# Attention maxima reduced two banks at a time, with four banks for maxima and two for scores

## The reference

```python
q = _split_heads(x @ qw + qb)
k = _split_heads(ctx @ kw + kb)
v = _split_heads(ctx @ vw + vb)
scores = jnp.einsum('bqhd,bkhd->bhqk', q, k) / np.sqrt(D // H).astype(np.float32)
if mask is not None:
    scores = scores + mask
probs = jax.nn.softmax(scores, axis=-1)
out = jnp.einsum('bhqk,bkhd->bqhd', probs, v)
...
h = h @ w + b + residual      # then a layer norm
ca = _mha(input_tensor, ctx_tensor, ctx_attn_mask, ...)   # cross
sa = _mha(x, x, None, ...)                                # self, on the cross result
```

## Time and profile before

| what | us |
|---|---|
| median of three timed runs (2017.12 to 2017.86) | 2017.5 |
| the profiled execution's own time | 2010.88 |
| its span | 2009.2 |
| PE busy | 1782.9 (89%) |
| DVE busy | 1414.8 (70%) |
| ACT busy | 1221.4 (61%) |
| POOL busy | 1217.2 (61%) |
| mean granted TensorE clock | 0.947 |
| DVE reductions of line 711, 1024 of 684 ns | 650.5 |
| ACT exponentials of line 625, 1024 of 601 ns | 571.3 |

### The profile page before, as it was taken

One profiled execution on the slowest core, in us unless ns is written; L12 is line 12 of the kernel. 1 busy time (PEld: TensorE's weight loads), 2 busy tenths in 40 slices (PEclk: granted clock), 3 DMA queues, 4 the chain that ended last, 5 costly groups with the idle time before them and its releaser, 6 DMA issues. The chain is left out here.

```text
span 2009.2 us, 36355 instructions
## 1 busy us (share of the span) xinstructions
PE 1782.9 (89%) x12326; PEld 1320.8 (66%) x12326; DVE 1414.8 (70%) x2786; ACT 1221.4 (61%) x2305; POOL 1217.2 (61%) x1117
## 2 busy tenths in 40 slices
PE   0699699999999999996994999941999999999996
PEld 0355355555555555553543898841999999999995
DVE  5378578878787887885852789863766666666662
ACT  0167467767676776774772554512777777777773
POOL 6644475556657555554435365651778778878875
PEclk9799899999999999998997999965999999999998
DMA  3665356656555665643503022215666766766662
GB/s 91 118 136 106 88 102 137 136 114 143 113 129 98 137 137 113 139 111 69 119 31 113 31 83 88 85 72 177 226 218 216 224 218 216 222 220 216 222 219 39
DMA packets 125197, 274.80 MB, mean 137 GB/s; under 512 B 15802, under 2 KB 57914, under 8 KB 124628
## 3 DMA queue, kind: packets, MB, share of 16 engines
q1 hardware_dynamic: 110708, 253.77, 46.2%
q0 software_dynamic: 14304, 18.72, 4.6%
HBM read 196.50 MB, written 75.92 MB: 136 GB/s over the span
## 5 line engine op out<-in xcount | busy, mean ns | idle before, releaser
L711 DVE TENSOR_REDUCE nz<-ps 128x1 f32<-128x512 f32 x1024 | 650.5, 684 | 215.9 <-PE ps L849 214.0
L625 ACT ACTIVATE spare<-ps 128x512 f32<-128x512 f32 x1024 | 571.3, 601 | 296.9 <-PE ps L859 292.6
L1747 POOL TENSOR_TENSOR u_lo<-u_f,u_hi 128x256 fp32r<-128x256 f32 x273 | 378.8, 1398 | 145.4 <-ACT u_hi L1781 144.0
L1853 PE MATMUL ps_e<-x_hi,we_hi 128*128 128x256 f32 x1092 | 312.8, 286 | 4.9 <-DVE we_lo L1667 4.9
L1853 PE MATMUL ps_e<-x_lo,we_hi 128*128 128x256 f32 x1092 | 305.6, 280 | 0.0
L1853 PE MATMUL ps_e<-x_hi,we_lo 128*128 128x256 f32 x1092 | 305.5, 280 | 0.0
L859 PEld LDWEIGHTS ps<-qst,kst 52*128 52x128 f32 x1024 | 101.7, 184 | 278.1 <-ACT spare L625 192.4
L871 PE MATMUL ps<-spare,vaug 128*32 128x512 f32 x2048 | 275.3, 610 | 0.0
L859 PE MATMUL ps<-qst,kst 52*128 52x512 f32 x1024 | 269.2, 502 | 3.8 <-ACT spare L625 3.5
L849 PE MATMUL ps<-kst,qst 50*128 50x512 f32 x1024 | 263.9, 441 | 9.1 <-issue 8.3
L1707 DVE TENSOR_TENSOR u_f<-ps_e,silu 128x256 f32<-128x256 f32 x273 | 115.1, 422 | 182.5 <-ACT silu L1812 181.3
(11 more groups left out here) (224 smaller groups left out, 3612.3 us busy)
## 6 DMA issues: line engine op xcount, KB each, us to landing
we_raw<-in_experts_w SPq DMA_DIRECT2D x117, 896.0 KB, 4.9
parts_kept<-parts SPq DMA_DIRECT2D x64, 512.0 KB, 3.9
kst<-parts_kept SPq DMA_DIRECT2D x192, 128.0 KB, 4.5
qst<-parts_kept SPq DMA_DIRECT2D x192, 128.0 KB, 5.2
x_raw<-xs SPq DMA_DIRECT2D x39, 259.0 KB, 2.8
maxima<-nsplit SPq DMA_DIRECT2D x64, 128.0 KB, 2.9
x<-sum_tok SPq DMA_DIRECT2D x16, 512.0 KB, 2.7
x_tok<-x SPq DMA_DIRECT2D x16, 512.0 KB, 4.0
```

Source lines behind the costliest of these rows:

```text
L625: act.activation(probs[:, e % 8], ps[:, score_bank(e, par)], ACT.Exp, scale=SCALE).then_inc(exp_made, 1)
L711: dve.tensor_reduce(nz[:, g % 2, place:place + 1], ps[:, max_bank(m, par)], AX.X, ALU.max, negate=True).then_inc(max_made, 1)
L1747: pool.tensor_tensor(u_lo[:, it], u_f[:, q % UPS], u_hi[:, it].bitcast(F32), ALU.subtract).then_inc(ulo_made, 1)
L1853: ins = pe.matmul(ps[:, q % UPS, c * GR:(c + 1) * GR], left, right, start=m == 0, stop=m == len(terms) - 1)
```

## The change

There are four banks for maxima and two for scores. DVE reduces the two heads of a pair in one instruction, which reads two banks and writes two maxima for each query, and raises its semaphore by two. It waits for the second product of the pair.

```diff
-SCORE_BANKS, MAX_BANKS, MISC_BANKS = 3, 3, 1
+SCORE_BANKS, MAX_BANKS, MISC_BANKS = 2, 4, 1
...
             def reduce_max(u, m, par):
-                g, i, qt, half = max_place(m)
+                g, i, qt, _ = max_place(m)
                 if m % 16 == 0 and positive(u * NG + g - 1):
                     dve.wait_ge(nz_turned, u * NG + g - 1)
-                dve.wait_ge(max_mm, u * 64 + m + 1)
-                place = qt * 32 + 2 * half + i
-                dve.tensor_reduce(nz[:, g % 2, place:place + 1], ps[:, max_bank(m, par)], AX.X,
-                                  ALU.max, negate=True).then_inc(max_made, 1)
-                if m % 16 == 15:
+                dve.wait_ge(max_mm, u * 64 + m + 2)
+                place = qt * 32 + i
+                bank = max_bank(m, par)
+                dve.tensor_reduce(nz[:, g % 2, place:place + 3:2], ps[:, bank:bank + 2], AX.X,
+                                  ALU.max, negate=True).then_inc(max_made, 2)
+                if m % 16 == 14:
                     turn_max(u, g)
...
-                for m in range(LEAD):
+                for m in range(0, LEAD, 2):
                     reduce_max(0, m, 0)
...
-                    for m in (2 * s + LEAD, 2 * s + LEAD + 1):
-                        if m < 64:
-                            reduce_max(u, m, par)
-                        elif after:
-                            reduce_max(u + 1, m - 64, 1 - par)
+                    m = 2 * s + LEAD
+                    if m < 64:
+                        reduce_max(u, m, par)
+                    elif after:
+                        reduce_max(u + 1, m - 64, 1 - par)
```

## The result

The changed kernel takes 2061.0 us (median of four, 2060.2 to 2061.7) against 2017.7 before (2017.1 to 2024.7): a ratio of 1.0206, with a 95% interval of 1.0183 to 1.0229. It is slower by 43 us; forecast were 37. Its profiled execution took 2061.66 us with a span of 2059.9, so that the two spans differ by 50.7 us. Of the 50.7 some 7 are luck, as the kernel before took 2010.9 in its profile against a median of 2017.7; in the 13 runs beside e7_turn_late it took 2010.7 to 2020.8.

The account below looks back on a forecast made before the run. PE was taken as the bound, with about 42 us of DVE waits over it. Score waits less DVE waits gave +49 us, less 12 given back, +37 on 2017.5: 2054 us, range for 8 in 10 2028 to 2084.

Parts of the forecast that it names:

- What bounds: In attention, PE is the bound, with about 42 us of DVE waits over the kernel, 2.5 us a period.
- The reductions: On DVE, one reduction over two banks takes 1.21 us (bounds 1.14 and 1.37); some 4 us a period relieved, hidden.
- Maxima with four banks: In attention periods, four banks for maxima take off nearly the whole DVE wait: 2.5 us a period.
- The start: At the start, 34 maxima reduced in pairs in place of singly: about 1 us less.
- Scores with two banks: In attention periods, score loads wait for the exponential two back: 5.5 us a period more, bounds 0.23 and 8.
- The sum: Over the kernel, lost score waits less DVE waits won: +49 - 12 = +37 us; 3.0 us for a full period.
- What is given back: At POOL's waits and token reloads, PE's later arrival shortens existing waits: 12 us off the +49.
- the 7 at POOL's waits: At five period starts PE waits less for POOL's last split of a normalised input: 5 x 1.4 = 7 us off.
- the 5 where tokens are reloaded: Twice PE stands some 15 us for tokens reloaded in a hurry; later arrival there gives 5 us back.
- The last period: In the last period, half without maxima: eight times 0.35 us and 1.7 for its first half, +4.5 us.
- Rival 3: Clock drops in attention, mean 0.98 to 0.92, from many short waits: +55 us on top, 2109; chance 6%.
- The rule that the forecast set aside: In attention, short PE idles from cycling banks can swing the clock, costing more than the sum; the trace's tail didn't show it.

Follow-up runs that it names:

- e7_turn_late: The kernel of e5 with DVE's transposition of 16 finished maxima moved behind the first reduction of the next slot: 2006.5 us, ratio 0.9957.
- e4: The kernel before, three and three banks, with each reduction reading only the first 256 of its 512 columns: 1986.3 us, ratio 0.985.
- e1: The banks of the change (two for scores, four for maxima), but DVE reduces one bank in each instruction, as before: 2058.9 us, ratio 1.0198.
- e2: The kernel before with two score banks instead of three, three for maxima, one bank unused, single reductions: 2078.7 us, ratio 1.0304.
- e3: The changed kernel with ACT's copy out of the MISC bank moved behind the second exponential of the slot: 2032.3 us, ratio 1.0068.
- e5: The kernel before with DVE's scaling of an output or sum of a projection moved between a slot's two reductions: 2003.4 us, ratio 0.9937.
- e6: The changed kernel with unread products of maxima added on PE in the last period, DVE unchanged: 2058.4 us, ratio 1.0206.

## Why the prediction was right

- *What bounds.* PE in order, with DVE's waits on it: right. Without these waits a period took 55.1 us (e4), and 55.0 was the sum of its shortest slots. The 42 us read from the view of waits were 31 in the time, and it is partly luck that they fit 16 periods of 2.5: 27 of the 74 waits lie in the start phase, and the 47 in the periods (9.8 us of idle) give 24 us by the same sum. In period 8 they are the 0.5 each of slots 0, 18 and 24; 0.22 of the 2.5 is the late score of slot 27, and the rest are slots 0.13 to 0.15 longer (5, 6, 17, 23, 29, 31), which e4 also brings to their shortest length.
- *The reductions.* 1.222 us for 1.21, and without effect, as said (e1). DVE was relieved of 1.6 us a period (48.78 to 47.21), not of some 4: two reductions in a row had taken 1.29 us and not twice 0.684, as the earlier trace rows show.
- *Maxima with four banks.* The waits went but for the start: right. With two score banks they are worth 20 us (e2 against e1) and not 31, as score waits hide a part. The start was put at -1 us and the first score came 0.6 later; in the nine profiles it came between 99.6 and 102.7, so this term can't be judged.
- *Scores with two banks.* 0.58 behind k and q (0.58 or 0.59 measured), 0.49 behind v (0.50), 0.42 behind a light slot that follows an output item (0.41 and 0.39), 1.2 in the last five slots (1.2). The sum gave 60.5 and the period took 60.45. e3 shows that it is this round trip: with the copy moved, what it holds up is gone.
- *What is given back.* Periods 1 to 13 took 28.5 us more; the sum had 39 less 12. Of the 12, the 7 at POOL's waits were 8.5, and the 5 where tokens are reloaded were 2. The five odd periods from 3 to 11 took 1.4 to 2.9 us more than a full one, and now 0.4. Two of them, 3 and 9, took most, because there the granted clock stood at 0.50 for 3.4 us too (from 294.3 and 645.9), and in the change it doesn't fall there. At the start of period 7, PE waits 0.40 us now, 1.41 before:

```profile
544.85 0.47 PE L784 MATMUL ps<-ctx_hi,w_hi 128*128 128x512 f32 x1 [0.40 <-issue]
```

  It goes the other way too. As PE gets there sooner in e4 and e5, slot 0 of period 7 takes 4.96 and 5.64 us (4.23 before, 2.71 after). That is a reason why 2.4 us a period made only 31 us, and it lowers what any gain in the period is worth. e4 shows a second one: in slot 15 of period 2 PE stands before the first maximum of the next period, which waits for its keys and queries, and the slot took 2.69 us in place of 1.67.
- *The last period* was the term that was mis-sized: +4.5 forecast, +10.7 measured. Its first 14 slots took 1.1 us more (1.7 forecast) and the rest 9.5 (2.8 forecast). At full clock two thin slots take 3.1 us in the change (16 and 17) against 2.6 to 2.7, as forecast 3.0; eight of them at 3.1 would have made about 4. The other 5.6 are an estimate of what the clock cost, which fell to half speed for 17 us; two thin slots took 4.55 us there. e6 bounds it from below with 3.0. The sum had no term for it. Rival 3 had the clock falling in full periods, where it never did (1.00 in period 8), and took the tail of the earlier trace rows as evidence that it would hold there. It held with three score banks and fell with two. The busy time doesn't warn of it: in the 8.5 us ahead of the fall PE is busy 7.2 (39 products, 1069.7 to 1078.2), and 7.3 (41 products) at the same place of the last period in the kernel before (1033.3 to 1041.8), where the clock stays at 1.00. In all the profiles with two banks and no filler (the change, e1, e2, e3) it stood at half for 14 to 27 us in the last period; in those with three (before, e4, e5, e7) not once there. PE in order of time, in the stretch at half speed, shows the price: a group of values takes 1.94 us from first start to last end, and 1.06 at full clock (at 1057.57).

```profile
1081.54 1.28 PE L860 MATMUL ps<-qst,kst 52*128 52x512 f32 x2 [0.69 <-ACT spare L625]
1082.75 1.94 PE L872 MATMUL ps<-spare,vaug 128*32 128x512 f32 x8
```

  The rule that the forecast set aside, in the Trainium skill (TensorE: Matmul & The Clock Gate, "A second HAM failure mode: psum-queue depth-cycling"), that short idles from cycling through banks can swing the clock, agrees with the last period of this kernel and not with its full ones, nor with e6_filler, which cycles through two score banks with waits of the same length and keeps 1.00.
- *The sum.* +37 from +49 - 12, and +43 timed. Between the profiles it was 50.7: 28.5 in periods 1 to 13, 0.6 before the first score, 4.1 in period 0, 3.2 in period 14, 10.7 in the last up to its last pair of scores, and 3.7 behind it, where the GELU stage started with 37.5 us at half clock against 23.9 before. The last part was not forecast and no run here takes it apart; e4, with three score banks, has 37.5 us there too, so two score banks are not needed for it.

## What to carry to other kernels

Before banks are taken from one consumer for another, write down the round trip of each (product, wait, read, release) with whatever stands between two reads in the consumer's queue, and hold it against the shortest slot of the producer: here 1.68, 2.16 and 2.25 us against 1.26 and 1.67 gave the result to 0.1 us a period. A wait by an engine that works in order is paid in full by all that stands behind it, so where waits for a bank are short, first move what holds up its release: one item placed between the reductions and not ahead of them gave 0.6%, no bank taken from anyone.

## What the runs showed of the hardware

- A DVE reduction from PSUM over 1024 elements in two banks takes 1.222 us, over 512 in one 0.684, over 256 0.419: 1.04 to 1.05 ns an element and about 0.15 us for each instruction. Crossing into a second bank costs under 0.01 us, as the step from 256 to 512 elements has the same price an element.
- The granted clock of TensorE fell to 0.50 for 17 us in the last period of the change and stayed at 1.00 there when PE had products added (e6). PE is shown busy 15.6 of 17.0 us in both, with 55 products at the half clock and 92 at the full one: products last longer at the half clock, so a busy time inside such a stretch says little of the work in it.
- One kernel on one chip varied by 10 us (2010.7 to 2020.8) from run to run; full periods within one profile repeated within 0.05 us (57.44 to 57.48 before, 60.46 to 60.47 in the change).
